# Twelve of 439 neighbour tiles fetched row by row from two other queues, and lane one-hots compared with an iota in PSUM

## The reference

```python
x = x + _L0_gnn_ref(_layernorm(x), edge_index, edge_attr_16, ...)   # per edge: relu([x_i, x_j, e] @ mW1 + mb1) @ mW2, summed by node
x = x + _L0_ffn_ref(_layernorm(x)[None], ...)[0]                    # shared MLP + two of four experts
x = x + _L1_gnn_ref(_layernorm(x), edge_index, ...)                 # two SAGE convolutions
x = x + _L1_ffn_ref(_layernorm(x)[None], ...)[0]                    # gelu FFN on the better half of the nodes

def _sage_conv(x, src, tgt, W_l, b_l, W_r):
    agg = segment_sum(x[src], tgt) / max(deg, 1)
    return agg @ W_l + b_l + x @ W_r
```

## Time and profile before

| what | value |
|---|---|
| median of 3 runs | 2928.23 us (2925.83 to 2932.85) |
| the profiled execution | 2927.9 us, span of the records 2926.1 us |
| granted TensorE clock, mean | 0.915 |
| busy: PE, DVE, POOL, ACT | 2337.2, 1870.9, 1804.0, 1030.2 us |
| record DMAs of the sort, L419 | 416, 451.8 us busy, mean 1086 ns |
| neighbour gathers of the second sum, L1909 | 439, 415.2 us busy, mean 946 ns |
| lane one-hots, L729 | 52, 1214/1215/1220 ns (min, median, max) |
| column one-hots, L722 | 52, mean 3821 ns |

### The profile page before, as it was taken

One profiled execution on the slowest core, in us unless ns is written; L12 is line 12 of the kernel. 1 busy time (PEld: TensorE's weight loads), 2 busy tenths in 40 slices (PEclk: granted clock), 3 DMA queues, 4 the chain that ended last, 5 costly groups with the idle time before them and its releaser, 6 DMA issues. The chain is left out here.

```text
span 2926.1 us, 34808 instructions
## 1 busy us (share of the span) xinstructions
PE 2337.2 (80%) x8554; PEld 1421.9 (49%) x8554; DVE 1870.9 (64%) x3838; ACT 1030.2 (35%) x2853; POOL 1804.0 (62%) x1842
## 2 busy tenths in 40 slices
PE   5488898229999999998998887888876655556799
PEld 2144443115555555555666664555454433334577
DVE  8897785217777777774544456666645444444898
ACT  1177878217677777662222221000030000000232
POOL 5777777777677676761006566777747777777200
PEclk8799999559999999999999999999778788888899
DMA  9223225029999999996016565555344333333001
GB/s 282 75 62 105 85 87 173 14 65 271 261 270 267 262 266 265 265 264 211 28 56 207 160 200 173 167 169 168 104 124 124 105 106 105 106 105 106 19 1 45
DMA packets 229078, 433.58 MB, mean 148 GB/s; under 512 B 45882, under 2 KB 121292, under 8 KB 228686
## 3 DMA queue, kind: packets, MB, share of 16 engines
q0 software_dynamic: 93888, 248.27, 31.7%
q1 hardware_dynamic: 129504, 177.80, 18.4%
q10 hardware_dynamic: 5488, 5.28, 0.5%
HBM read 310.36 MB, written 122.99 MB: 148 GB/s over the span
## 5 line engine op out<-in xcount | busy, mean ns | idle before, releaser
L958 POOL DMA_INDIRECT qg<-q_d,rb x480 | 479.0, 998 | 207.3 <-issue 103.5
L419 POOL DMA_INDIRECT recs_d<-recs,slot_src x416 | 451.8, 1086 | 146.1 <-issue 132.3
L1909 POOL DMA_INDIRECT nbr_yg<-y_d,gidx x439 | 415.2, 946 | 156.7 <-issue 86.8
L1075 PE MATMUL p_sum<-hb,wide 128*96 128x512 f32 x960 | 451.9, 593 | 1.2 <-ACT hb L1004 1.1
L1004 ACT ACTIVATE hb<-hb 128x512 f32<-128x512 f32 x480 | 297.1, 630 | 205.2 <-DVE hb L1044 201.2
L1748 POOL DMA_INDIRECT nbr_yg<-y_d,gidx x298 | 282.4, 948 | 94.4 <-issue 57.6
L1044 DVE TENSOR_TENSOR hb<-p_h,qg 128x512 f32<-128x512 f32 x480 | 312.6, 680 | 35.3 <-DMA qg<-q_d,rb 31.4
L1349 POOL DMA_INDIRECT n_ahead<-y_d,gidx x141 | 134.8, 956 | 268.8 <-DMA y_d<-n_y 198.5
L443 ACT ACTIVATE lane_hot<-bare_hot,val 128x128 f16<-128x128 f16 x832 | 247.5, 391 | 130.4 <-DVE bare_hot L729 130.1
L1845 PE MATMUL nbr_sum<-nbr_yg,nbr_hot 128*128 128x258 f32 x596 | 215.9, 460 | 67.8 <-DMA nbr_yg<-y_d,gidx 55.8
L1030 DVE SCALAR_TENSOR_TENSOR agg<-agg,keep,p_sum 96x512 f32<-96x512 f32 x240 | 178.1, 742 | 123.3 <-PE p_sum L1075 122.4
(11 more groups left out here) (377 smaller groups left out, 4084.6 us busy)
## 6 DMA issues: line engine op xcount, KB each, us to landing
agg_d<-agg SPq DMA_DIRECT2D x240, 192.4 KB, 5.0
msg_d<-n_ahead SPq DMA_DIRECT2D x141, 128.0 KB, 2.7
nbr_ys<-msg_d SPq DMA_DIRECT2D x141, 128.0 KB, 2.7
nbr_yg<-y_d,gidx POOLq DMA_INDIRECT x737, 2.8
p_low<-p_d SPq DMA_DIRECT2D x11, 768.0 KB, 12.5
recs_d<-fill SPq DMA_DIRECT2D x16, 510.0 KB, 17.5
rb<-recs_d SPq DMA_DIRECT2D x60, 136.0 KB, 5.1
qg<-q_d,rb POOLq DMA_INDIRECT x480, 5.7
```

The source lines that it names most:

```text
L419: pool.indirect_dma_start(S.recs[:, :], bass.IndirectOffsetOnAxis(ap=slot_src[:, c:c + 1], axis=0), recs[:, c, :], None).then_inc(s_scat, 16)
L958: pool.indirect_dma_start(qg[t % QB][:, :], None, S.q[:, :], bass.IndirectOffsetOnAxis(ap=rb[n % RB][:, t % BT, 1:2].bitcast(U32), axis=0) ...
L1075: last = pe.matmul(p_sum[g % 2][0:SB, :], wide[g % XB][:, j, 0:SB], hb[t % HB][:, :], start=(j == 0), stop=(j == 1))
L1909: pool.indirect_dma_start(yg[t % GB][:, 0:D], None, S.y[0:EARLY_NODES, :] if t < NSTORED else S.y[:, :], bass.IndirectOffsetOnAxis(ap=C.gi ...
```

## The change

Two edits that have nothing to do with each other.

*Lane one-hots.* One copy puts the numbers 0 to 63 into the 64 columns of the PSUM bank `p_iota` behind the column iota. `bare_hot` is then made in two instructions of 64 lanes each, (iota + 0 or 64) == lane, where one instruction compared 128 lanes with the iota in SBUF.

*Neighbour tiles.* Tiles 361, 367, ..., 427 leave POOL's list. SP fetches the six from 361 to 391, ACT the six from 397 to 427. For each of the 128 partitions they load that partition's six indices into registers and issue six DMAs of one row (1 KB) each, into twelve buffers of their own. The rows of three tiles share one semaphore, and since the loop over partitions is the outer one, all six tiles of an engine are complete only after its last partition. PE waits for them when it comes to their tile. POOL gathers the remaining 427.

```diff
+        lane_row = p_iota[:, NCOL:NCOL + P // 2]
...
+            step.link(dve.tensor_copy(lane_row, C.iota_f[:, 0:P // 2]))
...
-            lane_iota = C.iota_f[:, :].rearrange("p (a n) -> p a n", a=1)
+            lane_iota = lane_row.rearrange("p (a n) -> p a n", a=1)
...
-                dve.tensor_tensor(bare_hot[g % BARE][:, :, :], lane_iota.to_broadcast([P, TC, P]),
-                                  lane[:, TC * g:TC * g + TC].rearrange("p (c a) -> p c a", a=1).to_broadcast([P, TC, P]),
-                                  ALU.is_equal).then_inc(s_bare, 1)
+                for half in range(2):
+                    last = dve.scalar_tensor_tensor(
+                        out=bare_hot[g % BARE][:, :, half * P // 2:(half + 1) * P // 2],
+                        in0=lane_iota.to_broadcast([P, TC, P // 2]), scalar=float(half * P // 2),
+                        in1=lane[:, TC * g:TC * g + TC].rearrange("p (c a) -> p c a", a=1).to_broadcast([P, TC, P // 2]),
+                        op0=ALU.add, op1=ALU.is_equal)
+                last.then_inc(s_bare, 1)
...
+        BY_ROWS, ROWS_AT, APART = 6, 361, 6
+        by_rows = {ROWS_AT + APART * n: n for n in range(2 * BY_ROWS)}
+        rows_of = [m.sb(f"rows{n}", [P, W]) for n in range(2 * BY_ROWS)]
+        s_rows = [m.sem(f"rows{n}") for n in range(4)]
+        by_tiles = [t for t in range(NTILE) if t not in by_rows]
...
+        def gather_rows(eng, side):
+
+            for b in range(YB):
+                eng.wait_ge(s_yst[b], 16 * len(range(b, NT, YB)))
+            first = ROWS_AT + APART * BY_ROWS * side
+            for p in range(P):
+                rows = load_own_buckets(nc, eng, C.gidx[p:p + 1, first:first + APART * (BY_ROWS - 1) + 1:APART].bitcast(I32),
+                                        NPAD - 1)
+                for n in range(BY_ROWS):
+                    eng.dma_start(rows_of[BY_ROWS * side + n][p:p + 1, 0:D], S.y[bass.ds(rows[n], 1), :]
+                                  ).then_inc(s_rows[2 * side + n // (BY_ROWS // 2)], 16)
...
                     sp.dma_start(dst, src, allow_slow_non_contiguous=True).then_inc(s_last, 16)
+                gather_rows(sp, 0)
...
-                for t in range(NTILE):
+                for n, t in enumerate(by_tiles):
...
-                    if t >= GB:
-                        pool.wait_ge(s_sum, t - GB + 1)
+                    if n >= GB:
+                        pool.wait_ge(s_sum, by_tiles[n - GB] + 1)
...
+                gather_rows(act, 1)
...
+                    if t in by_rows:
+                        n = by_rows[t]
+                        pe.wait_ge(s_rows[n // (BY_ROWS // 2)], 16 * P * (BY_ROWS // 2))
+                        rows = rows_of[n]
```

More of the change, by code:

```diff
@@ L1874, in stage_second_neighbours @@
         assert len(s_gath) == GB // PER
+        BY_ROWS, ROWS_AT, APART = 6, 361, 6
[3 more added lines that the diff above has]
+        by_tiles = [t for t in range(NTILE) if t not in by_rows]
+        place_in = {t: n for n, t in enumerate(by_tiles)}
+        assert max(by_rows) < NTILE and BY_ROWS % 2 == 0
+        def gather_rows(eng, side):
[8 more added lines that the diff above has]
+                                  ).then_inc(s_rows[2 * side + n // (BY_ROWS // 2)], 16)
         of_projection = [tr.full, tr.empty, out.full, out.empty, s_deg, s_deg_at, s_h, s_x] + s_yst
@@ L1890, in _ @@
                     sp.dma_start(dst, src, allow_slow_non_contiguous=True).then_inc(s_last, 16)
+                gather_rows(sp, 0)
                 sp.wait_ge(s_last, 16 * 6)
                 sp.wait_ge(s_acc, NSTORED + 1)
+                sp.wait_ge(s_rows[2], 16 * P * (BY_ROWS // 2))
                 for sem in of_projection:
@@ L1899, in _ @@
                     pool.memset(yg[b][:, D:W], 1.0).then_inc(s_zero, 1)
+                for n in range(2 * BY_ROWS):
+                    pool.memset(rows_of[n][:, D:W], 1.0).then_inc(s_zero, 1)
                 for b in range(YB):
                     pool.wait_ge(s_yst[b], 16 * len(range(b, EARLY_NODES // P, YB)))
-                for t in range(NTILE):
+                for n, t in enumerate(by_tiles):
                     if t == NSTORED:
@@ L1905, in _ @@
                             pool.wait_ge(s_yst[b], 16 * len(range(b, NT, YB)))
-                    if t >= GB:
-                        pool.wait_ge(s_sum, t - GB + 1)
+                    if n >= GB:
+                        pool.wait_ge(s_sum, by_tiles[n - GB] + 1)
                         pool.nop(nofuse=True)
-                    pool.indirect_dma_start(yg[t % GB][:, 0:D], None, S.y[0:EARLY_NODES, :] if t < NSTORED else S.y[:, :],
+                    pool.indirect_dma_start(yg[n % GB][:, 0:D], None, S.y[0:EARLY_NODES, :] if t < NSTORED else S.y[:, :],
                                             bass.IndirectOffsetOnAxis(ap=C.gidx[:, t:t + 1], axis=0)
-                                            ).then_inc(s_gath[t // PER % len(s_gath)], 16)
+                                            ).then_inc(s_gath[n // PER % len(s_gath)], 16)
             @block.scalar
@@ L2029, in _ @@
                     last.then_inc(out.full, 1)
-                pe.wait_ge(s_zero, GB)
+                pe.wait_ge(s_zero, GB + 2 * BY_ROWS)
                 for t in range(NTILE):
@@ L2041, in _ @@
                         pe.wait_ge(s_acc, t - SUMS + 2)
[L2042 to L2045, removed]
+                    if t in by_rows:
+                        n = by_rows[t]
+                        pe.wait_ge(s_rows[n // (BY_ROWS // 2)], 16 * P * (BY_ROWS // 2))
+                        rows = rows_of[n]
+                    else:
+                        n = place_in[t]
+                        if n % PER == 0:
+                            b = n // PER % len(s_gath)
+                            pe.wait_ge(s_gath[b], C.gathered[b] + 16 * (PER * (n // GB) + min(PER, len(by_tiles) - n)))
+                        rows = yg[n % GB]
+                    pe.matmul(p_sum[t % SUMS][:, 0:W], hot[t // BT % HOTS][:, t % BT, :], rows[:, :], start=True,
                               stop=True).then_inc(s_sum, 1)
```

## The result

The changed kernel takes **2964.27 us** (median of 4 runs, 2960.81 to 2967.81), against 2930.1 us for the kernel before on the same chip: 1.0118 times as long, interval 1.0097 to 1.0139. The change costs 34 us; the forecast was a gain of 57. The profiled execution is the longest of the four, 2967.81 us, with a span of 2966.0.

A forecast was written before the change was run, and what follows sets the result against it. Every stage adds its length, set by the engine ending last: POOL in the sort and the second neighbour sum. 2927.9 us less 42 (edit 1) and 15 (edit 2) gave 2871 us, range 2862 to 2922.

The forecast's parts named there:

- The bound of the sort, and edit 1: Sort ends with POOL; new one-hots no longer hold its record DMAs (1148 to 969 ns), gaining 42 us.
- POOL never catches up with the gate: Sort: 20 record DMAs take 25.4 us, the three groups that advance the gate 22.5, so POOL does not wait.
- When the rows are wanted: Second neighbour sum, tile 361: rows complete by 2639 us keep the full 15.0 us gain, gone at 2654.
- T: Time when the fetched rows are complete, forecast 2636.5 us; the stage ends at the later of 2706.6 and T + 67.7.
- When they come: SP's row fetches: six-number load 0.32 us, partition 3.41 us, rows complete at 2636.5 us, in time by 2.5 us.
- The prediction's own sign of being wrong: SP and ACT row fetches: wrong if row DMAs start over 0.55 us apart or register loads take over 0.5 us.
- Rows somewhat late: Rival, row fetches: loads take 0.6 to 0.73 us, edit 2 costs 17 to 35 us, 2903 to 2921 us; chance 0.22.
- Each row costs the back-to-back price: Rival, wait before tile 361: a partition takes 4.5 us, deciding from 3.93; 121 us lost, 3007 us; chance 0.12.
- SP and ACT take turns: Rival, row fetches: one queue's DMA keeps the other's out, 42 us lost, 2928 us, no change; chance 0.07.
- The new one-hots hold POOL: Rival, sort: record DMAs stay held, edit 1 brings nothing, 2913 us; chance 0.09.

The follow-up runs named there:

- edit 1 alone: Only the lane one-hots changed against the kernel before, all 439 neighbour tiles left to POOL: 2902.9 us against 2933.0, ratio 0.9895.
- edit 2 alone: Only the twelve tiles fetched by rows against the kernel before, lane one-hots as before: 3003.23 us against 2933.0, ratio 1.0239.
- The kernel with aligned loads: Changed kernel with index columns copied into eight aligned columns per queue, six used, all eight loaded: 2885.86 us against 2930.44 for the kernel before, ratio 0.9837.

## Why the prediction was wrong

*The bound of the sort, and edit 1: right, 42 us was 30.* The record DMAs went to 986 ns, the hold is gone. Over all 416 the mean fell from 1086 to 985 ns in the changed kernel, which is the 42 us (to 988 and 41 us in the run with edit 1 alone). But POOL's idle time before them grew: for PE's `acc` from 1.8 us to 9.7 in that run and 4.6 in the changed kernel, so the step "POOL never catches up with the gate" was wrong, by up to 8 us. The records come 32 us earlier in that run and 35 in the changed kernel. By the medians the kernel keeps 30. DVE's lane one-hots took 0.681 us, against 0.67, and were covered.

*When the rows are wanted: right.* Gathers stayed 1.25 us apart. The stage was to end at T + 67.7; it ended at T + 67.9 in the changed kernel and at T + 66.7 with edit 2 alone. With the rows in time the gathers' 15 us came, as 14.7, and 13.4 of them reached the stage's end.

*When they come: wrong, and this failed the prediction.* The step reads "I take 0.32, since the row nearest to this loop, a load between DMAs with their address work, is the fast one." Six numbers six columns apart take 1.56 us. By 0.30 + 0.20 a number the load is 1.50. The row of DVE that the step went by the earlier trace rows is not one of eight numbers, as its heading has it. It mixes loads of one, three, five and eight, and its median of 0.604 is the price of eight from a multiple of four (in the second sum eight take 0.60 us and one takes 0.31). Its maximum of 1.198 was left unread: it is the price of five numbers that begin elsewhere, paid 36 times in that trace by the first neighbour sum alone. Six numbers at no less than 1.18 us would have made a partition 3.05 + 1.18 + 0.04 = 4.27 us and T = 2746, and edit 2 a loss. So the bounds of 0.32 and 0.73 were taken from runs that begin at a multiple of four, and they don't bound six strided numbers.

A partition took 4.12 us instead of 3.41, T was 2694; the forecast's 2636.5, less the 28 us by which this trace's gathers began earlier, is 2608. The prediction's own sign of being wrong, register loads of over 0.5 us, came true. Two terms were put too high, in the other direction: a row, with 0.225 us for the DMA and (4.12 - 1.56)/6 = 0.43 us from row to row instead of 0.509, and the landing, 2.7 us after the last DMA, where PE goes on at 2694.01 us as the last DMA starts at 2694.0, since its tile needs only the first three rows of a partition. The kernel with aligned loads runs in 2886 us; of the 15 us above 2871 edit 1 has 12, and the stage and the spread of the runs the rest.

The Trainium skill, Runtime: NRT & Kernel Launch, section Instruction fetch mechanics, gives about 200 ns a register for a register load. The page speaks of loads from HBM and the loads here read SBUF, but the trace agrees with the figure where numbers are fetched one by one: 0.20 us each, beside a fixed 0.30. The Trainium skill, DMA: Bandwidth & Descriptors, section Latency and other measured facts, gives about 600 ns as the floor of such a load. The rows go below it, with 0.27 to 0.51 us for one number, and they decide. An estimate of 1.2 us for six numbers, by the first page's figure, would have put T at 2749 us in the prediction's sum and made edit 2 a loss.

*The rivals.* "Rows somewhat late" had the right place and too small a delay. "Each row costs the back-to-back price" had the right sign, the deciding point (3.93 us a partition, exceeded by 4.12) and the wrong mechanism: not the DMA, the load. "SP and ACT take turns" didn't happen: with both queues full, SP's DMAs took 0.225 and ACT's 0.235 us, their medians being within 1 ns of their minima. 473 of SP's 768 overlap one of ACT's in time, and the median of those is 0.225 us too. "The new one-hots hold POOL" fell.

## What to carry to other kernels

Work that goes to idle queues has to be costed per instruction in the shape that it will really have. If the trace has only a relative of it, that is no bound until one knows what the price depends on, and a row whose minimum, median and maximum are as far apart as 307, 604 and 1198 ns has to be taken apart by what each instruction loads. Where an edit has a date (rows wanted by 2639 us), the margin a partition, here 0.02 us, says how well a price must be known: if it hangs on an instruction that the trace doesn't show, that one is to be measured first. Numbers that a queue reads into registers belong side by side, in groups of four from a multiple of four. Two small copies turned the loss of 34 us into a gain of 45, of which edit 1 has 30.

## What the runs showed of the hardware that was not expected

A register load pays 0.20 us for each number beside 0.30 us, unless the run starts at a multiple of four numbers: then four cost 0.23 us together (six from column 360: 0.96 us, from 361: 1.50). That is SP and ACT beside the second neighbour sum; on DVE five numbers take 1.18 us, or 0.59 from a multiple of four. Something else moves the price too: one number takes 0.51 us there and took 0.276 in the node stage, and SP's loads of four in the edge network, all from multiples of four, took 0.298 to 1.011 us, while PE's 60 of the same shape beside them had a median of 0.332. What that is stays open. A record DMA on POOL that starts under a lane one-hot with both inputs in SBUF is held until this one ends, less 0.12 us, so two instructions of half the size held it for 0.53 us at most instead of 1.05. And one chip ran the kernel before 12% slower (3292.86 against 2930 us) and the row DMAs far more than that (four in 9.89 us); its cause was not found.
